# Moving the token blocks' reciprocals and products, and TensorE's transposes, to later units of an attention loop

## The chip, the cores and the metric

The kernel runs on one core of one Trainium2 chip. The metric is the device time of one execution in microseconds (us); lower is better. The core's engines work from instruction lists of their own and signal each other through semaphores: TensorE (PE in the profile; PEld are its weight loads), VectorE (DVE), ScalarE (ACT), GpSimd (POOL) and the transfer queue SyncE (SP).

## The reference, cut to what matters

```
x  : 8 x 512 tokens of 256 numbers;  xn = layernorm(x)
q, k, v = xn @ W_qkv.T                      16 heads of 16 numbers
qp, kp  = elu(q @ proj) + 1, elu(k @ proj) + 1     128 features a head
kv   = kp^T v  (per head, over the 512 tokens)     ksum = sum of kp
attn = (qp kv) / (qp ksum + 1e-8)
x + attn @ W_out.T + b_out + mixture of experts(xn)   8 experts, the best two of each token
```

The mixture of experts is the second half of the kernel and is not touched by the change.

## The kernel before, in words

The attention part goes through the 8 blocks of 512 tokens, one turn of a loop for each: block 0 is written out (`first=True`), blocks 1 to 6 are the turns of a loop, block 7 is `final_iteration`. Each engine has its own `iteration`, and a turn consists of 32 units, u = 0 to 31. Unit u makes one 128x512 piece of features: TensorE's `unit` multiplies it into PSUM bank F[u % 4] (L529 for the k features, u < 16, L535 for the q features), ScalarE's `exp` (L959) writes the exponential into the ring e_ring of four, and VectorE's `features` (L1355) combines both into kp or qp. TensorE's unit u waits until feature u-4 is done (semaphore `feat`), ScalarE's exp(u) also waits for feature u-4.

Everything else of the loop is hung between the units by hand, at an `if u == ...` of each engine. In turn b this is the state product of block b (`kv`, L547, 4 groups of 32 records, one for each 128 tokens), the projections of block b+1 (`qk_group` and `v_logits`, L473 to L475; `qk_rest`, L499, which subtracts the rounded part so that ScalarE's `qk_lo`, L938, can read what is left), and the end of block b-1: the attention result att_sb is transposed to tokens (`to_tokens`, L576, one for each of the four token blocks n = 0 to 3), VectorE takes the reciprocals of the denominators (`reciprocals`, L1361, 128x16) and multiplies (`products`, L1367, 128x256), and TensorE transposes back (`to_heads`, L583) and projects.

What ties these together are the PSUM banks that they share. `to_tokens(n)` writes the banks WK[1], DEN, WK[0], NUM for n = 0 to 3. `v_logits(b + 1, 0)` writes WK[1] and so waits for product 0 (`at_rdy` 4b-3), `kv(b, 0)` writes DEN and waits for product 1 (4b-2), `qk_group(b + 1, 1)` writes WK[0] and waits for product 2 (4b-1), `to_heads` needs all four products (4b). `to_tokens(b - 1, 3)` writes NUM and waits until `qk_lo(b + 1, 0)` has read it (`qkl_rdy` 4b+5). Feature 8 overwrites the kp half that `kv(b, 0)` reads, and waits for it (`kv_done`). On ScalarE, `qk_lo(b + 1, 0)` stands behind exp(11) and ahead of exp(12).

GpSimd sends the rows of block b to the experts' lists with eight indirect transfers (L1713) in each turn. They are paced by TensorE: transfer j waits until unit 2j is signalled (`f_full`, `TURN = 2`). SyncE loads x, xres and stores the result in the first third of a turn and rearranges kd and qd into Sk and Sq later.

Of the kernel before, what the change touches and what calls it, by code (L numbers as in the profile page):

```python
# [72 lines left out]
def build(nc, x, w_in, proj, w_out, b_out, experts, b1, b2, br, consts, out):  # L73
# [396 lines left out]
    def _(pe):  # L470
        def mm3(dst, wh_, wl_, mh_, ml_, first, last):

            nc.tensor.matmul(dst, wh_, mh_, start=first, stop=False)  # L473
            nc.tensor.matmul(dst, wh_, ml_, start=False, stop=False)  # L474
            return nc.tensor.matmul(dst, wl_, mh_, start=False, stop=last)  # L475
# [10 lines left out]
        def qk_group(b, i):  # L486

            pe.wait_ge(xtl_rdy, 2 * b + 2)
            col = (D, D + P, 0, P)[i]
            for k in range(KT):  # L490
                last = mm3(QK_BANK[i][:, :], WTh[:, k, col:col + P], WTl[:, k, col:col + P],
                           xTh[:, k, :], xTl[:, k, :], k == 0, k == KT - 1)
            last.then_inc(qk_full, 1)
# [8 lines left out]
        def v_logits(b, n):  # L502

            pe.wait_ge(xtl_rdy, 2 * b + 2)
            tok = slice(n * P, (n + 1) * P)
            for k in range(KT):
                last = mm3(V_BANK[n][:, 0:D + E], xTh[:, k, tok], xTl[:, k, tok],
                           WTh[:, k, 2 * D:QKVR], WTl[:, k, 2 * D:QKVR], k == 0, k == KT - 1)
            last.then_inc(v_full, 1)
# [29 lines left out]
        def kv(b, n):  # L539

            pe.wait_ge(feat, 32 * b + 4 * n + 4)
            if n == 0:
                pe.wait_ge(v_rdy, NT * b + NT)
            for c in range(4):
                for j in range(4):
                    h = 4 * c + j
                    last = nc.tensor.matmul(KV[32 * j:32 * j + 32, c * P:(c + 1) * P], vext[:, n, h, :],  # L547
                                            kp[:, n % 2, h * FEAT:(h + 1) * FEAT],
                                            start=n == 0 and c == 0, stop=n == NT - 1, skip_group_check=True)
            last.then_inc(kv_done, 1)  # L550
# [62 lines left out]
        def iteration(b, first=False):  # L613
# [4 lines left out]
            for u in range(32):  # L618
# [20 lines left out]
                    to_tokens(b - 1, 2)  # L639
                if u == 5:  # L640
                    qk_group(b + 1, 0)
                if u == 7:
                    if not first:
                        pe.wait_ge(at_rdy, 4 * b - 3)
                    v_logits(b + 1, 0)
                    if first:
                        pe.wait_ge(pos_read, 1)
                    else:
                        pe.wait_ge(at_rdy, 4 * b - 2)
                    kv(b, 0)  # L650
# [3 lines left out]
                if u == 13:  # L654
                    if not first:
                        pe.wait_ge(at_rdy, 4 * b - 1)
                    qk_group(b + 1, 1)
                    pe.wait_ge(qkl_rdy, 4 * b + 5)
                    if not first:
                        to_tokens(b - 1, 3)  # L660
# [534 lines left out]
    def _(dve):  # L1195
# [8 lines left out]
        def join():  # L1204
            dve.wait_ge(step, chain[0] + chain[1])
# [186 lines left out]
        def iteration(b, first=False, ahead=True):  # L1392
            for u in range(32):
                if u == 0:
                    norm_rows(b + 1, 0, 4)
                if u == 2:
                    tokens_lo(b + 1, 0)
                    tokens_lo(b + 1, 1)
                if ahead:
                    if u == 16:  # L1400
                        norm_stats(b + 2, 0, 2)
                    if u == 17:
                        norm_stats(b + 2, 2, 4)
                        join()
                    if u == 18:
                        norm_var(b + 2)
                    for i in STEPS_AT.get(u, ()):
                        norm_step(b + 2, i)
                if u == 27:
                    route_top(b + 1)  # L1410
                    route_mask(b + 1)
                    route_count(b + 1)
                if u == 28:
                    route_weights(b + 1)
                if u == 31:
                    numbers_of(b + 1)
                if not first:
                    if u == 3:
                        reciprocals(b - 1, 0)
                        reciprocals(b - 1, 1)  # L1420
                        products(b - 1, 0)
                    if u == 4:
                        products(b - 1, 1)
                    if u == 8:
                        reciprocals(b - 1, 2)
                    if u == 10:
                        products(b - 1, 2)
                    if u == 14:
                        reciprocals(b - 1, 3)
                        products(b - 1, 3)  # L1430
                    if u == 30:
                        residual(b - 1, 0)
                    if u == 31:
                        residual(b - 1, 1)
                if u == 31:
                    slots_of(b + 1)
                features(b, u)
# [383 lines left out]
```

## Time and profile before

| | us |
|---|---|
| median of 3 runs | 748.63 (747.15 to 756.17) |
| profiled execution | 756.15 |
| its span, first to last instruction | 754.0 |
| mean granted clock of TensorE | 0.986 |

| engine | busy us | share of the span |
|---|---|---|
| PE | 704.2 | 93% |
| PEld | 619.9 | 82% |
| DVE | 492.8 | 65% |
| ACT | 476.4 | 63% |
| POOL | 221.2 | 29% |

The page divides the span into 40 slices; the attention turns of the blocks 1 to 6 lie from about 66 to 287 us, and one turn takes 36.8 us. The views in order of time give the start of an instruction or of a merged group of equal ones, its length, engine, line, what it writes and reads, the count, and in brackets the idle time of the engine just before it with what ended that.

### The profile page before, as it was taken

What the parts mean: (1) busy time and instruction counts of PE and PEld (TensorE: products, weight loads), DVE (VectorE), ACT (ScalarE), POOL (GpSimd) and SP (SyncE); (2) the same over time, 40 slices, a digit from 0 to 9 for tenths busy, and PEclk for the clock granted to TensorE, in tenths of its full rate; (3) what the DMA queues carried; (4) which work ended last, traced back from release to release, by engine and by line L of the source; (5) the groups of instructions that cost most, each with busy time, mean ns of one, the idle gap of its engine ahead of it and who ended that gap; (6) DMA issues with size and microseconds to landing.
All of it is one profiled execution on the core that took longest, in us unless ns stands there. A gap on an engine that the chain in (4) does not pass through costs nothing.

```text
span 754.0 us, 17665 instructions
## 1 busy us (share of the span) xinstructions
PE 704.2 (93%) x5589; PEld 619.9 (82%) x5590; DVE 492.8 (65%) x1279; ACT 476.4 (63%) x879; POOL 221.2 (29%) x165
## 2 busy tenths in 40 slices
PE   3898999999999998799999999999999999999995
PEld 2675776767767675469999999999999999999995
DVE  7788888888889787936466464455656444456442
ACT  3587878686969696855556765546675444566551
POOL 0232323323232324522232422224222223322322
PEclk9899999999999999989999999999999999999998
DMA  7765464746473637643544642225445223443421
GB/s 232 183 185 143 116 197 113 204 106 205 104 211 98 183 98 214 219 156 89 139 88 87 155 150 50 43 44 101 150 76 154 43 52 69 82 112 86 59 43 22
DMA packets 50181, 91.64 MB, mean 122 GB/s; under 512 B 6897, under 2 KB 30193, under 8 KB 47873
## 3 DMA queue, kind: packets, MB, share of 16 engines
q1 hardware_dynamic: 34402, 59.36, 27.9%
q0 software_dynamic: 13872, 18.75, 14.3%
q10 hardware_dynamic: 1872, 13.11, 4.9%
q8 instruction: 17, 0.28, 0.2%
q14 instruction: 18, 0.15, 0.1%
HBM read 39.32 MB, written 26.67 MB: 88 GB/s over the span
## 4 chain that ended last, share of the span: by engine, by line
PE 64%; DVE 13%; issue 8%; ACT 8%; another core or an unknown queue 2%; DMA 1%; ACTq 1%; SPq 1%; DVEq 0%; POOLq 0%
PE F L473 9%; PE F L475 8%; PE F L474 8%; PE NUM L473 3%; PE F L529 3%; PE NUM L474 3%; PE NUM L475 3%; DVE qp L1355 3%; ACT h L1114 3%; ACT e_ring L959 3%; PE DEN L474 3%; PE DEN L473 3%; PE DEN L475 3%; PE F L535 2%; PE WK L567 2%
## 5 line engine op out<-in xcount | busy, mean ns | idle before, releaser
L1114 ACT ACTIVATE h<-F,b1c 128x384 f32<-128x384 f32 x200 | 110.8, 575 | 163.9 <-PE F L475 156.2
L1772 POOL DMA_INDIRECT out<-ysb,icur x75 | 120.0, 1599 | 303.7 <-DVE ysb L1616 288.9
L1593 DVE TENSOR_TENSOR hl<-h,hh 128x768 fp32r<-128x768 f32 x100 | 95.9, 959 | 156.7 <-ACT hh L1118 156.7
L959 ACT ACTIVATE e_ring<-F 128x512 f32<-128x512 f32 x256 | 145.3, 622 | 47.8 <-PE F L529 40.8
L473 PE MATMUL F<-gxh,wh 128*128 128x384 f32 (+1 forms) x400 | 129.8, 325 | 3.9 <-ACT h L1114 1.7
L475 PE MATMUL F<-gxh,wl 128*128 128x384 f32 (+1 forms) x400 | 128.4, 321 | 0.0
L474 PE MATMUL F<-gxl,wh 128*128 128x384 f32 (+1 forms) x400 | 128.4, 321 | 0.0
L1713 POOL DMA_INDIRECT xg<-rows,slots x64 | 63.2, 987 | 192.7 <-PE F L529 183.3
L1355 DVE SCALAR_TENSOR_TENSOR kp<-F,e_ring 128x512 f32<-128x512 f32 x128 | 82.5, 683 | 20.5 <-ACT e_ring L959 18.8
L1355 DVE SCALAR_TENSOR_TENSOR qp<-F,e_ring 128x512 f32<-128x512 f32 x128 | 85.3, 684 | 5.9 <-ACT e_ring L959 4.9
L1118 ACT ACTIVATE hh<-h 128x768 fp32r<-128x768 f32 x100 | 84.7, 847 | 3.3
L473 PEld LDWEIGHTS F<-gxh,wh 128*128 128x128 f32 x400 | 75.8, 190 | 9.1 <-issue 6.2
L474 PEld LDWEIGHTS F<-gxl,wh 128*128 128x128 f32 x400 | 75.9, 190 | 0.0
L475 PEld LDWEIGHTS F<-gxh,wl 128*128 128x128 f32 x400 | 75.8, 190 | 0.0
L529 PEld LDWEIGHTS F<-stacked_proj,Sk 97*128 97x128 f32 x256 | 37.3, 196 | 31.5 <-issue 15.2
L535 PE MATMUL F<-Sq,stacked_proj 97*128 97x512 f32 x128 | 54.0, 453 | 8.5 <-DVE qp L1355 5.6
L473 PE MATMUL NUM<-wh,hh 128*128 128x256 f32 x200 | 59.2, 296 | 1.8 <-DVE hl L1593 1.8
L529 PE MATMUL F<-stacked_proj,Sk 97*128 97x256 f32 x256 | 48.8, 310 | 8.7 <-DVE kp L1355 4.6
L473 PE MATMUL DEN<-wh,hh 128*128 128x256 f32 x200 | 56.6, 283 | 0.0
L474 PE MATMUL DEN<-wl,hh 128*128 128x256 f32 x200 | 56.6, 283 | 0.0
L475 PE MATMUL DEN<-wh,hl 128*128 128x256 f32 x200 | 56.6, 283 | 0.0
L475 PE MATMUL NUM<-wh,hl 128*128 128x256 f32 x200 | 56.4, 282 | 0.0
(220 smaller groups left out, 1572.6 us busy)
## 6 DMA issues: line engine op xcount, KB each, us to landing
wraw<-experts ACTq DMA_DIRECT2D x12, 1024.0 KB
grow<-xg SPq DMA_DIRECT2D x26, 408.0 KB
Sk<-kdh SPq DMA_DIRECT2D x64, 128.0 KB, 2.8
Sq<-qdh SPq DMA_DIRECT2D x64, 128.0 KB
xin<-x SPq DMA_DIRECT2D x8, 512.0 KB
Sk<-kdl SPq DMA_DIRECT2D x32, 128.0 KB, 2.5
Sq<-qdl SPq DMA_DIRECT2D x32, 128.0 KB
xres<-x SPq DMA_DIRECT2D x8, 512.0 KB
```

The source lines that it names most:

```text
L473: nc.tensor.matmul(dst, wh_, mh_, start=first, stop=False)
L474: nc.tensor.matmul(dst, wh_, ml_, start=False, stop=False)
L475: return nc.tensor.matmul(dst, wl_, mh_, start=False, stop=last)
L529: last = nc.tensor.matmul(F[c][:, s * D:(s + 1) * D], Sk[0:SROWS, pr, n * P:(n + 1) * P], stacked_proj[0:SROWS, 2 * pr:2 * pr + 2, :], sta ...
L535: last = nc.tensor.matmul(F[h % 4][:, :], stacked_proj[0:SROWS, h, :], Sq[0:SROWS, h // 2, :], start=True, stop=True)
L959: A(e_ring[:, u % 4, :], F[u % 4][:, :], ACT.Exp, bias=EXP_BIAS, scale=1.0 / DOWN).then_inc(exp_done, 1)
L1114: A(h32[:, m, :], F[m % 4][:, 0:T], ACT.Gelu, bias=b1c[:, w, m:m + 1]).then_inc(gelu, 1)
L1118: A(hh[:, 2 * q:2 * q + 2, :], h32[:, 2 * q:2 * q + 2, :], ACT.Copy).then_inc(hh_rdy, 1)
L1355: V.scalar_tensor_tensor(dst, F[u % 4][:, :], DOWN, e_ring[:, u % 4, :], ALU.max, ALU.min).then_inc(feat, 1)
L1593: V.tensor_tensor(hl[:, 2 * q:2 * q + 2, :], h32[:, 2 * q:2 * q + 2, :], f32(hh[:, 2 * q:2 * q + 2, :]), ALU.subtract).then_inc(hl_rdy, 1)
L1713: pool.indirect_dma_start(xg, bass.IndirectOffsetOnAxis(slots[:, k:k + 1], 0), rows[:, n, :], None, bounds_check=last_row, oob_is_err=Fals ...
L1772: pool.indirect_dma_start(out, bass.IndirectOffsetOnAxis(icur[:, s, :], 0), ysb[:, s, :], None, bounds_check=last_token, compute_op=ALU.ad ...
```

## The change

In VectorE's list of the blocks 1 to 6, the reciprocals of the token blocks 0 and 1 and product 0 move from ahead of feature 3 to ahead of feature 6, product 1 from 4 to 7, reciprocals 2 from 8 to 9, reciprocals 3 and product 3 from 14 to 17; product 2 stays at 10. In TensorE's list of the blocks 0 to 6, `v_logits(b + 1, 0)` moves from behind unit 7 to behind unit 8, `kv(b, 0)` from behind unit 7 to behind unit 9, and `to_tokens(b - 1, 3)` with its wait for `qk_lo` from behind unit 13 to behind unit 15. Nothing is added or removed, and block 7's turn stays.

```diff
--- before.py
+++ after.py
@@ -639,10 +639,11 @@
                     to_tokens(b - 1, 2)
                 if u == 5:
                     qk_group(b + 1, 0)
-                if u == 7:
+                if u == 8:
                     if not first:
                         pe.wait_ge(at_rdy, 4 * b - 3)
                     v_logits(b + 1, 0)
+                if u == 9:
                     if first:
                         pe.wait_ge(pos_read, 1)
                     else:
@@ -655,6 +656,7 @@
                     if not first:
                         pe.wait_ge(at_rdy, 4 * b - 1)
                     qk_group(b + 1, 1)
+                if u == 15:
                     pe.wait_ge(qkl_rdy, 4 * b + 5)
                     if not first:
                         to_tokens(b - 1, 3)
@@ -1415,17 +1417,17 @@
                 if u == 31:
                     numbers_of(b + 1)
                 if not first:
-                    if u == 3:
+                    if u == 6:
                         reciprocals(b - 1, 0)
                         reciprocals(b - 1, 1)
                         products(b - 1, 0)
-                    if u == 4:
+                    if u == 7:
                         products(b - 1, 1)
-                    if u == 8:
+                    if u == 9:
                         reciprocals(b - 1, 2)
                     if u == 10:
                         products(b - 1, 2)
-                    if u == 14:
+                    if u == 17:
                         reciprocals(b - 1, 3)
                         products(b - 1, 3)
                     if u == 30:
```

## Rows read from the trace of the kernel before

**Rows 1.** busy time by stretch, its columns and the stretch of blocks 1 to 6

```profile
core 0: us, PE busy (x) PEld busy (x) DVE busy (x) ACT busy (x) POOL busy (x), PEclk, DMA share, GB/s
...
66.00:287.00 221.00, 212.18 (x1947) 156.78 (x1945) 188.19 (x561) 171.52 (x366) 68.51 (x61) 1.00 0.55 152
```

**Rows 2.** TensorE in time, block 4's turn: start, length, line, operation, count, idle before

```profile
182.15 0.50 PE L529 MATMUL F<-stacked_proj,Sk 97*128 97x256 f32 x2 [0.58 <-DVE kp L1355]
...
183.31 1.08 PE L547 MATMUL DEN<-kp,vext 128*32 128x128 f32 x32
184.32 1.20 PE L529 MATMUL F<-stacked_proj,Sk 97*128 97x256 f32 x8
185.45 1.08 PE L547 MATMUL DEN<-kp,vext 128*32 128x128 f32 x32
186.46 0.50 PE L499 MATMUL NUM<-kdh,minus 128*128 128x512 f32 x1
...
189.24 0.65 PE L576 MATMUL NUM<-cst,att_sb 128*128 128x128 f32 x4 [0.32 <-ACT kdl L938]
...
190.54 1.10 PE L535 MATMUL F<-Sq,stacked_proj 97*128 97x512 f32 x2 [0.17 <-DVE kp L1355]
...
194.83 0.60 PE L583 MATMUL WK<-cst,at 128*128 128x128 f32 x4
```

**Rows 3.** VectorE in time, the same turn, same columns

```profile
180.97 0.26 DVE L1361 RECIPROCAL rec<-DEN 128x16 f32<-128x16 f32 x1 [0.77 <-PE WK L576]
181.14 0.36 DVE L1367 TENSOR_TENSOR at<-WK,rec 128x256 f32<-128x256 f32 x1
181.42 0.68 DVE L1355 SCALAR_TENSOR_TENSOR kp<-F,e_ring 128x512 f32<-128x512 f32 x1
...
182.34 2.48 DVE L1355 SCALAR_TENSOR_TENSOR kp<-F,e_ring 128x512 f32<-128x512 f32 x4
...
185.58 1.29 DVE L1355 SCALAR_TENSOR_TENSOR kp<-F,e_ring 128x512 f32<-128x512 f32 x2 [0.60 <-ACT e_ring L959]
...
189.80 1.29 DVE L1355 SCALAR_TENSOR_TENSOR kp<-F,e_ring 128x512 f32<-128x512 f32 x2 [1.40 <-ACT e_ring L959]
191.00 0.25 DVE L1361 RECIPROCAL rec<-NUM 128x16 f32<-128x16 f32 x1
...
194.07 0.74 DVE L1241 BATCH_NORM_STATS2 stats<-xin 128x6 f32<-128x256 f32 x2
```

**Rows 4.** ScalarE in time, the same turn, same columns

```profile
184.86 2.06 ACT L959 ACTIVATE e_ring<-F 128x512 f32<-128x512 f32 x4 [1.57 <-PE F L529]
188.59 0.60 ACT L938 ACTIVATE kdl<-NUM 128x512 fp32r<-128x512 f32 x1 [1.67 <-remote]
189.09 1.08 ACT L959 ACTIVATE e_ring<-F 128x512 f32<-128x512 f32 x2
```

**Rows 5.** GpSimd in time, the same turn, same columns

```profile
182.37 0.98 POOL L1713 DMA_INDIRECT xg<-rows,slots  x1 [2.19 <-PE F L529]
185.63 0.98 POOL L1713 DMA_INDIRECT xg<-rows,slots  x1 [2.27 <-PE F L529]
186.91 0.98 POOL L1713 DMA_INDIRECT xg<-rows,slots  x1 [0.30 <-issue]
```

**Rows 6.** waits over the whole run: waiter, releaser, us in total, times, longest

```profile
ACT kdl L938 <- remote: 9.9, 6, 1.7
...
DVE rec L1361 <- PE WK L576: 5.2, 6, 1.6
```

**Rows 7.** GpSimd in time, block 0's turn

```profile
41.57 0.99 POOL L1713 DMA_INDIRECT xg<-rows,slots  x1 [0.31 <-issue]
...
44.85 0.99 POOL L1713 DMA_INDIRECT xg<-rows,slots  x1 [0.30 <-PE F L529]
```

**Rows 8.** ScalarE in time, block 0's turn

```profile
43.28 0.60 ACT L938 ACTIVATE kdl<-NUM 128x512 fp32r<-128x512 f32 x1 [1.18 <-PE NUM L499]
...
45.21 2.10 ACT L959 ACTIVATE e_ring<-F 128x512 f32<-128x512 f32 x4
```

## The prediction

> **What bounds the kernel now.** Only the attention turns of the blocks 0 to 6 are edited, so I read, in this order: the busy time by stretch, to see which engine is full there; the timelines of TensorE, VectorE, ScalarE and GpSimd over one turn, to find TensorE's gaps and what ends each; the list of waits, to see that they come back in every turn. In the stretch of the blocks 1 to 6 TensorE is busy for 212.2 of 221.0 us and its clock is whole, 1.00 [rows 1]; VectorE has 188.2 and ScalarE 171.5. TensorE is the bound, and the change can only win what TensorE stands still, about 9 us in six turns, 1.5 a turn.
>
> In the turn of block 4 the stops are these. Unit 7 comes 0.58 late, for feature 3 [rows 2]. Feature 3 was late because VectorE stood for 0.77 ahead of reciprocal 1, for TensorE's `to_tokens` [rows 3]. Then `to_tokens(3)` comes 0.32 late, for ScalarE's kdl, and unit 16 0.17 late, for feature 12 [rows 2]. These two have one cause: ScalarE starts kdl at 188.59, after 1.67 of idleness [rows 4], though the matmul it waits for, `qk_rest`, ran from 186.46 to 186.96 by its record [rows 2]. The signal is 1.6 late. kdl stands ahead of exp(12) (189.09 [rows 4]), so feature 12 starts at 189.80 after 1.40 of idleness [rows 3], and unit 16 waits for it. The first wait is seen 6 times with 5.2 us in all, the second 6 times with 9.9 [rows 6]: once in each turn.
>
> What makes TensorE's signal late? The view names no source. GpSimd issues an indirect transfer in 0.98, and in this turn two of them stand back to back, 185.63 and 186.91, 0.30 apart [rows 5]; they are the transfers paced by unit 8 and unit 10, which TensorE makes in one stretch (184.32, 8 records [rows 2]). The second ends at 187.89, and the signal gets through at 188.59, 0.70 later. In block 0's turn a pair ends at 42.56 [rows 7] and kdl starts at 43.28, again after a long wait, 0.72 after that end [rows 8]. So the working reading is that a pair of issues back to back holds TensorE's signals back until some 0.7 after its end. Against it: the next pair of block 0 (the second from 44.85 to 45.84 [rows 7]) leaves the four exponentials from 45.21 on without a gap [rows 8]. The Trainium skill, Perfetto Trace Analysis, "Tensor Engine Instruction (MATMUL, LD_WEIGHTS)", says that the end of a matmul in a profile is computed and that the signal is pushed once PSUM has acknowledged the writes, outside of the record. By that alone the 1.6 would belong to the matmuls and would move with them; that is the second case below.
>
> **The change part by part.** The work is the same to the instruction, and no transfer of SP or POOL is moved in its list; only GpSimd's issues shift, since units pace them. All times are of block 4's turn.
>
> VectorE, features 3 to 7. The stop of 0.77 goes: reciprocal 1 now comes three features later, and its signal is there by 180.97. A feature takes 0.60 from start to start (0.62: 2.48 for four [rows 3]). Features 3 to 5 follow the second from 179.95 (180.97 less the stop and 0.25 for reciprocal 0) to 181.75. Then two reciprocals (0.17 to 0.26 apart) and product 0 (0.36, [rows 3]) end at 182.50, feature 6 starts at 182.45, product 1 ends at 183.45, feature 7 at 184.05.
>
> TensorE, units 7 to 9. Unit 7 starts at 181.57 (182.15 less 0.58), unit 8 at 181.85; a unit takes 0.28 (1.13 for four, 184.32 to 185.45 [rows 2]). `v_logits` then waits for product 0, until 182.55: a new wait of about 0.4, queued behind it unit 9 and `kv(0)`. Before it began at 182.49 (it takes 0.82 up to 183.31 [rows 2]). Unit 9 at 183.37, `kv(0)` at 183.65, which takes 1.01 (185.45 to 186.46), units 10 and 11, `kv(1)` at 185.22 instead of 185.45. Most of the 0.58 is paid back in the new wait: 0.23 is left.
>
> VectorE, features 8 to 12. Feature 8 waited for exp(8), which waited for unit 8 behind `kv(0)` (184.86, idle 1.57 [rows 4]), and began at 185.58 [rows 3]. Now unit 8 is early and feature 8 waits for `kv(0)` only: 184.8. Product 2 ends about 186.65, before `qk_group(1)` wants its bank at 187.0, so the moved reciprocal costs nothing there; feature 11 ends by 187.8, half a microsecond sooner.
>
> GpSimd. The transfer of unit 6 stays at 182.37 [rows 5]. Unit 8 is signalled at 182.1, so its transfer follows back to back, about 183.65 to 184.63. The one of unit 10 comes some 0.77 after its signal (as 184.86 to 185.63, [rows 4, 5]), at 185.75 or, if the new pair holds signals until 185.3, at 186.1; unit 12's at 187.7. The pair across `qk_rest` is gone. The new pair can hold the signal of `kv(0)`, to 185.3 instead of 184.8; that delays feature 8 by 0.5 and `qk_group(1)` by 0.1.
>
> The signal of `qk_rest` then comes at its record's end, 186.73: kdl from 186.75, exp(12) from 187.25, feature 12 from 187.9 to 188.6. TensorE is no longer stopped: `qk_group(1)` 187.05 to 188.55, units 14 and 15 (0.56), `to_tokens(3)` (0.43), unit 16 at 189.6 instead of 190.54. With these new waits about 0.9 is won a turn.
>
> Reciprocals and product 3. They stood between features 13 and 14 (191.00) and now follow the second pair of statistics (194.07, 0.74 long [rows 3]). Without them ahead that pair ends at 194.18, and product 3 at 194.9 (0.25 + 0.42), signalled at about 194.95; `to_heads` started at 194.83 [rows 2]. If feature 12 stays where it is, this costs 0.1 a turn; if feature 12 is 1.9 earlier, as above, product 3 is ready long before `to_heads` (now about 193.9), and the move costs nothing. Putting `to_tokens(3)` behind units 14 and 15 lets these cover its wait (0.32); where the wait is gone anyway, the move is worth nothing by itself.
>
> Block 0's turn has the same signal, kdl at 43.28, but no reciprocals; its part, below 0.5, I leave in the range. Blocks after 7 and the experts do not change.
>
> Sum: 6 turns x 0.9 = 5.4 us. Of the span of 754.0 that leaves 748.6, of the profiled 756.15 it leaves 750.8. That execution stood 7.5 above the median of the runs, 748.63; taken from the median the sum gives 743.2.
>
> **The rivals.**
>
> *The late signal stays late.* If it does not hang on the pair of issues, kdl moves only with `kv(1)`, by 0.23 at most, and feature 12 and unit 16 with it; product 3 takes back up to 0.1. For it: the pair of block 0 without effect [rows 7, 8], and the page's reading above. Against it: in both turns looked at the delay ends 0.70 to 0.72 after the end of an issue. Price: -0.23 to +0.1 a turn, 747.2 to 749.2; I take 748.5.
>
> *The signal comes later than now.* Place: kdl again. If the new pair (units 6 and 8) holds the signals of units 10 and 11 as well, the transfers of units 8, 10 and 12 can close up, and the last ends at 188.3, its hold at 189.0. kdl would come 0.45 later, unit 16 as much, and product 3 a further 0.1 behind `to_heads`: 0.55 x 6 = 3.3, 751.9. It decides from a kdl at about 188.5 on. For it: the three gaps in the new schedule are small, 0.3, 1.1 and 0.6 to 0.9. Against it: the lone issue of 182.37 to 183.35 [rows 5] goes by without harm to `kv(0)` at 183.31 and the unit behind it [rows 2].
>
> *All stops go.* TensorE then loses 0.23 as above and all of 0.32, 0.17 and the 0.16 or so which the bracketed gaps leave out, 1.1 to 1.3 a turn with 0.5 in block 0: up to 8 us, 740.6.
>
> **How the numbers follow.** The forecast, with kdl's signal in time, has 0.47; the late signal that stays 0.31; later than now 0.17; all stops gone 0.05. The time is 743.2. The likeliest case by itself runs from 741 to 746. The range reaches over the others: 740.5 below, and above 752, the price of the slower case, which leaves out its tail and runs like the one of 756.17. Two per cent (15 us) is about what a measurement of this kernel can tell from no change. No case reaches it: the whole of TensorE's idleness in the six turns is 9 us. Faster by over 2% has 0.02, slower 0.03, for a wait that I did not find; the rest, 0.95, is within.
>
> **What would show it right or wrong.** In the profile after: no idle time ahead of the second reciprocal; unit 7 at once behind unit 6; a wait of VectorE's product ahead of `v_logits`, 0.3 to 0.5; GpSimd's issues of units 6 and 8 back to back, those of units 8 and 10 apart; kdl with little idle time ahead of it and not named remote; feature 12 without its 1.40; unit 16 and `to_heads` without a wait. A turn should take 35.9 instead of 36.8. If the list of waits still has kdl with 1.6 six times, the reading of the signal was wrong; if `to_heads` waits for product 3, VectorE's last move was put too late.

## The result and the profile after

| | before | after |
|---|---|---|
| median of 20 runs each, us | 752.23 (747.15 to 756.46) | 748.99 (743.54 to 751.88) |
| profiled execution, us | 756.15 | 749.08 |
| its span, us | 754.0 | 747.0 |
| turns of the blocks 1 to 6, one by one, us | 38.38 36.80 36.83 36.79 36.81 36.71 | 37.43 36.39 36.45 36.40 36.32 35.55 |

The ratio is 0.9947, with an interval of 0.9927 to 0.9967: 0.5% faster, 3.2 us between the medians, where 5.4 were forecast and, from the median of three runs, 743.2 in all. The turns in the middle have become 0.40 us shorter, not 0.9; the first and the last of the six are 0.95 and 1.16 shorter, which makes 3.8 in all. (A turn is counted from one end-of-turn `attend` to the next. Outside of these six turns an execution also differs from the next: block 7 takes 38.5 to 43.9 us over the traces of this document, and 38.5 and 40.9 in two of one kernel, while all that follows the last `attend` takes 426.8 to 427.2 in every one. So the length of a turn is the sharper measure, and the runs below are read by it.)

Busy time by stretch, the blocks 1 to 6 of the kernel after, in the columns of [rows 1]:

```profile
core 0: us, PE busy (x) PEld busy (x) DVE busy (x) ACT busy (x) POOL busy (x), PEclk, DMA share, GB/s
62.50:282.00 219.50, 212.51 (x1967) 158.84 (x1960) 189.86 (x564) 173.28 (x368) 69.03 (x62) 1.00 0.56 155
```

TensorE still stands 7.0 us in them (219.50 less 212.51), where it stood 8.8 before. To see where, TensorE in time, block 4's turn; 3.97 is added to a start to compare it with [rows 2 to 5] (the code lines below TensorE's part have moved on by 2: features is L1357, the reciprocals L1363, the products L1369, exp L961, kdl L940, the transfers L1715):

```profile
177.23 0.85 PE L529 MATMUL F<-stacked_proj,Sk 97*128 97x256 f32 x6
178.75 0.40 PE L473 MATMUL WK<-WTh,xTh 128*128 128x264 f32 x1 [0.66 <-DVE at L1369]
...
179.92 1.08 PE L547 MATMUL DEN<-kp,vext 128*32 128x128 f32 x32
...
181.58 1.08 PE L547 MATMUL DEN<-kp,vext 128*32 128x128 f32 x32
182.59 0.50 PE L499 MATMUL NUM<-kdh,minus 128*128 128x512 f32 x1
...
184.79 0.63 PE L529 MATMUL F<-stacked_proj,Sk 97*128 97x256 f32 x4
185.26 0.60 PE L576 MATMUL NUM<-cst,att_sb 128*128 128x128 f32 x4
185.66 1.09 PE L535 MATMUL F<-Sq,stacked_proj 97*128 97x512 f32 x2
...
190.47 0.63 PE L583 MATMUL WK<-cst,at 128*128 128x128 f32 x4 [0.36 <-DVE at L1369]
```

The three stops of before [rows 2] are gone: units 6 to 8 run as one, `to_tokens(3)` and unit 16 follow without a wait. Unit 16 stands at 189.63 in the time of before, against 190.54. But there are two new stops, both for a product of VectorE: 0.66 ahead of `v_logits` (product 0) and 0.36 ahead of `to_heads` (product 3), which comes at 194.44 against 194.83. VectorE in time, the same turn:

```profile
177.99 0.25 DVE L1363 RECIPROCAL rec<-WK 128x16 f32<-128x16 f32 x1
178.15 0.19 DVE L1363 RECIPROCAL rec<-DEN 128x16 f32<-128x16 f32 x1
178.26 0.42 DVE L1369 TENSOR_TENSOR at<-WK,rec 128x256 f32<-128x256 f32 x1
...
181.44 0.69 DVE L1357 SCALAR_TENSOR_TENSOR kp<-F,e_ring 128x512 f32<-128x512 f32 x1 [1.22 <-PE DEN L547]
...
184.91 2.67 DVE L1357 SCALAR_TENSOR_TENSOR kp<-F,e_ring 128x512 f32<-128x512 f32 x4 [0.54 <-issue]
...
188.74 0.74 DVE L1243 BATCH_NORM_STATS2 stats<-xin 128x6 f32<-128x256 f32 x2
189.61 0.26 DVE L1363 RECIPROCAL rec<-NUM 128x16 f32<-128x16 f32 x1
189.90 0.42 DVE L1369 TENSOR_TENSOR at<-NUM,rec 128x256 f32<-128x256 f32 x1
```

Reciprocal 1 no longer waits. Feature 8 waits 1.22 for `kv(0)` (and no more for exp(8)), feature 12 0.54. ScalarE and GpSimd around the signal of `qk_rest`:

```profile
183.70 0.60 ACT L940 ACTIVATE kdl<-NUM 128x512 fp32r<-128x512 f32 x1 [1.13 <-PE NUM L499]
```

```profile
178.43 0.98 POOL L1715 DMA_INDIRECT xg<-rows,slots  x1 [1.39 <-PE F L529]
179.71 0.98 POOL L1715 DMA_INDIRECT xg<-rows,slots  x1 [0.30 <-issue]
182.25 0.98 POOL L1715 DMA_INDIRECT xg<-rows,slots  x1 [1.55 <-PE F L529]
```

The pair of transfers is now that of units 6 and 8, as forecast, and a lone transfer lies over `qk_rest`. kdl starts 1.11 after `qk_rest` (183.70 less 182.59); before it was 2.13 (188.59 less 186.46, [rows 4] and [rows 2]). The waits over the whole run show how often this comes back:

```profile
DVE kp L1357 <- PE DEN L547: 9.2, 7, 1.5
ACT kdl L940 <- PE NUM L499: 6.3, 6, 1.2
...
PEld WK L473 <- DVE at L1369: 4.9, 6, 0.9
...
PE WK L583 <- DVE at L1369: 2.5, 6, 0.6
```

kdl's six waits are those of block 0 and of the turns 2 to 6. Turn 1 has none, and is worth a look by itself. TensorE's `qk_rest` and `to_heads`, ScalarE's kdl and GpSimd's issues around `qk_rest`, turn 1 of the kernel after:

```profile
73.21 0.50 PE L499 MATMUL NUM<-kdh,minus 128*128 128x512 f32 x1
...
81.24 0.63 PE L583 MATMUL WK<-cst,at 128*128 128x128 f32 x4 [0.61 <-DVE at L1369]
```

```profile
73.75 0.60 ACT L940 ACTIVATE kdl<-NUM 128x512 fp32r<-128x512 f32 x1 [0.17 <-issue]
```

```profile
70.74 0.98 POOL L1715 DMA_INDIRECT xg<-rows,slots  x1 [0.31 <-issue]
73.26 0.98 POOL L1715 DMA_INDIRECT xg<-rows,slots  x1 [1.54 <-PE F L529]
```

Here no issue is under way when `qk_rest` starts (the last one ended at 71.72, the next begins 0.05 after), and kdl follows after 0.54. In the other turns a lone issue has begun 0.15 to 0.52 before `qk_rest`, and kdl follows 1.00 to 1.23 after it, 0.41 to 0.52 after the end of that issue. Even with kdl in time `to_heads` waits 0.61 for product 3 in turn 1.

### The profile page after: what moved, and what is told of

Read it like the earlier page. It is cut to its first block, busy times and chain, and to the rows that moved or that the text cites. A ratio compares the mean times of both kernels' runs of the same rounds, so it can differ in the third digit from the quotient of the medians.

```text
span 747.0 us, 17664 instructions
## 1 busy us (share of the span) xinstructions
PE 697.9 (93%) x5589; PEld 616.6 (83%) x5590; DVE 492.5 (66%) x1279; ACT 476.1 (64%) x879; POOL 220.9 (30%) x165
## 4 chain that ended last, share of the span: by engine, by line
PE 61%; DVE 17%; issue 11%; ACT 7%; DMA 1%; ACTq 1%; DVEq 1%; POOLq 0%; SPq 0%; another core or an unknown queue 0%
PE F L473 9%; PE F L475 9%; PE F L474 9%; PE NUM L473 3%; DVE qp L1357 3%; PE NUM L474 3%; PE NUM L475 3%; DVE kp L1357 3%; ACT h L1116 3%; PE DEN L473 3%; PE DEN L474 3%; PE DEN L475 3%; PE DEN L547 2%; PE F L535 2%; PE WK L473 2%
## 5 line engine op out<-in xcount | busy, mean ns | idle before, releaser
L961 ACT ACTIVATE e_ring<-F 128x512 f32<-128x512 f32 x256 | 146.0, 624 | 43.1 <-PE F L529 36.3
L1715 POOL DMA_INDIRECT xg<-rows,slots x64 | 63.1, 985 | 184.8 <-PE F L529 173.8
L1357 DVE SCALAR_TENSOR_TENSOR kp<-F,e_ring 128x512 f32<-128x512 f32 x128 | 82.7, 681 | 18.6 <-PE DEN L547 9.2
L1357 DVE SCALAR_TENSOR_TENSOR qp<-F,e_ring 128x512 f32<-128x512 f32 x128 | 85.3, 683 | 6.4 <-ACT e_ring L961 6.0
L474 PE MATMUL NUM<-wl,hh 128*128 128x256 f32 x200 | 56.4, 282 | 0.0
```

What stands on the lines that cost most here:

```text
L961: A(e_ring[:, u % 4, :], F[u % 4][:, :], ACT.Exp, bias=EXP_BIAS, scale=1.0 / DOWN).then_inc(exp_done, 1)
L1357: V.scalar_tensor_tensor(dst, F[u % 4][:, :], DOWN, e_ring[:, u % 4, :], ALU.max, ALU.min).then_inc(feat, 1)
L1715: pool.indirect_dma_start(xg, bass.IndirectOffsetOnAxis(slots[:, k:k + 1], 0), rows[:, n, :], None, bounds_check=last_row, oob_is_err=Fals ...
```

## The experiments

The theory after these traces: the first half of the change (TensorE's `v_logits` and `kv(0)`, VectorE's reciprocals and products 0 to 2) and the second (`to_tokens(3)`, product 3) each take a stop away and put a new one in, and what is gained hangs on how late TensorE's signals come. The rival: the transfers, which the change shifts, decide. A signal is called in time here when its reader starts 0.54 us after the start of the 128x512 matmul that it waits for, and late when it starts later. The runs were made on chips numbered 4, 2, 9 and 0, each beside the kernel before on the same chip. The chip of the two first traces has no number on record; it is called the first chip, since the kernel before takes some 16 us longer there than on any of these.

**e1 and f3: the first half alone** (chips 4 and 2). **e2 and f4: the second half alone.** e1 and f3 take from the diff everything but its second hunk and the move of reciprocals 3 and product 3; e2 and f4 take these two alone:

```diff
                     qk_group(b + 1, 1)
+                if u == 15:
                     pe.wait_ge(qkl_rdy, 4 * b + 5)
...
-                    if u == 14:
+                    if u == 17:
                         reciprocals(b - 1, 3)
                         products(b - 1, 3)
```

> Only the first half of the change: reciprocals 0 and 1, products 0 and 1, reciprocals 2 on VectorE, v_logits and the first state product on TensorE; to_tokens(3), reciprocals 3 and product 3 stay as before. Theory S (the gain is the signal of qk_rest, which comes early because unit 8 and with it GpSimd's transfer moved away from it): kdl's wait falls from 1.67 to 1.1 or less a turn, unit 16 comes 0.9 sooner, and to_heads has no wait for product 3, since that stands where it stood: -0.9 a turn of six, about 5.5 us, ratio 0.992 to 0.994, better than the whole change. Rival (both halves are needed, since to_tokens(3) behind unit 13 still stops for kdl): -0.4 a turn, ratio 0.996 to 0.998.

> Only the second half of the change: to_tokens(3) behind unit 15, reciprocals 3 and product 3 ahead of feature 17. Theory S: kdl keeps its late signal, 1.67 a turn, feature 12 stays where it is, and to_heads now waits 0.1 to 0.4 for product 3: no gain, ratio 1.000 to 1.003. Rival (covering to_tokens(3)'s wait is what counts): -0.3 a turn, ratio 0.997 to 0.998.

Measured on chip 4: the kernel before 736.42 (19 runs), e1 740.85, ratio 1.0055 (1.0032 to 1.0079); e2 740.90, 1.0055 (1.0027 to 1.0082). Each half alone makes the kernel slower; e1 was expected to gain 5.5. That could not be understood without the kernel before itself on such a chip, 16 us faster there than on the first one. So:

> The kernel before once more, for a trace on the same chip as the runs beside it: the runs of the four experiments so far had 736.4 for it instead of 752.2, and no late signals in any of their traces up to feature 12. Theory C (whether signals are late depends on the chip, and all of the gain came from them): if its median here is near 736, kdl starts within 0.1 of the end of qk_rest and a turn takes 34.7 to 35.0; if near 750, kdl is 1.6 late and a turn takes 36.8. Rival (the time between chips differs for another reason, in the experts' part): the turn is 36.8 in both.

> The changed kernel, on the same chip. Theory C: where the kernel before takes about 736, v_logits' new wait for product 0 and feature 8's new wait for the state product are all that is left of the change, with to_heads' wait for product 3, so it is slower, ratio 1.006 to 1.012, a turn 35.6 to 35.9; where the kernel before takes about 750, ratio 0.993 to 0.996 as measured. Rival (the change wins everywhere): ratio 0.993 to 0.996 in both.

> The first half of the change again. Theory C: where the kernel before takes about 736, 1.004 to 1.007 as measured; where it takes about 750, kdl's signal is 0.6 late instead of 1.6, to_heads doesn't wait for product 3, ratio 0.990 to 0.994. Rival (the first half loses on every chip, the gain being the second half's): 1.004 or more in both.

> The second half of the change again. Theory C: where the kernel before takes about 736, 1.004 to 1.008 as measured, all of it to_heads' wait for product 3; where it takes about 750, kdl stays 1.6 late, feature 12 stays, 1.000 to 1.003. Rival (the second half brings the gain there, by covering the wait of to_tokens(3)): 0.994 to 0.997 where the kernel before takes about 750.

Measured on chip 2: before 736.58 (23 runs); f2, the whole change, 745.12, 1.0108 (1.0078 to 1.0137); f3 741.38, 1.0051 (1.0028 to 1.0074); f4 739.12, 1.0031 (1.0008 to 1.0055). The turns: before 34.64, whole change 36.0, first half 35.3, second half 35.4. The stretch of the blocks 1 to 6 in the kernel before on this chip (f1):

```profile
60.20:268.40 208.20, 206.85 (x1954) 156.96 (x1958) 189.98 (x568) 174.32 (x369) 67.50 (x60) 1.00 0.58 161
```

TensorE stands 1.35 us in six turns, not 8.8: here there is next to nothing to win. Its ScalarE and its GpSimd at `qk_rest`, which starts at 177.70:

```profile
178.24 0.60 ACT L938 ACTIVATE kdl<-NUM 128x512 fp32r<-128x512 f32 x1
```

```profile
176.89 0.98 POOL L1713 DMA_INDIRECT xg<-rows,slots  x1 [1.44 <-PE F L529]
178.17 0.98 POOL L1713 DMA_INDIRECT xg<-rows,slots  x1 [0.30 <-issue]
179.46 0.98 POOL L1713 DMA_INDIRECT xg<-rows,slots  x1 [0.30 <-issue]
```

kdl starts 0.54 after `qk_rest`, with no idle time ahead of it, although three transfers stand back to back across it, 0.30 apart. So a pair of issues by itself does not hold a signal back: as a rule for every chip the working reading of the prediction is refuted. On the first chip its traces bear it out in a wider form, a lone issue being enough. The nearest comparison is one kernel in two traces: in f2's block 4 an issue begins 0.37 before `qk_rest` and kdl starts 0.54 after it; in the trace of after on the first chip the issue begins 0.34 before (182.25 and 182.59) and kdl starts 1.11 after. Now the whole change on chip 2 (f2), TensorE in time, its two stops:

```profile
177.68 0.39 PE L473 MATMUL WK<-WTh,xTh 128*128 128x264 f32 x1 [0.47 <-DVE at L1369]
...
189.24 0.63 PE L583 MATMUL WK<-cst,at 128*128 128x128 f32 x4 [0.61 <-DVE at L1369]
```

They stand at the same two places as in the trace of after on the first chip. The next table puts block 4's turn side by side, us from the turn's start:

| | before, first chip | after, first chip | before, chip 2 | after, chip 2 | first half | second half |
|---|---|---|---|---|---|---|
| reciprocal 1 | 8.28 | 9.43 | 7.43 | 9.22 | 9.22 | 7.43 |
| `v_logits(0)` | 9.80 | 10.02 | 8.96 | 9.81 | 9.81 | 8.96 |
| `kv(1)` | 12.76 | 12.86 | 11.91 | 12.65 | 12.65 | 11.91 |
| kdl | 15.90 | 14.98 | 13.46 | 14.20 | 14.20 | 13.46 |
| unit 16 | 17.86 | 16.93 | 16.14 | 16.70 | 16.79 | 16.05 |
| product 3 | 18.60 | 21.18 | 16.27 | 20.80 | 16.90 | 20.15 |
| `to_heads` | 22.14 | 21.75 | 19.95 | 21.38 | 20.59 | 20.72 |
| turn | 36.79 | 36.40 | 34.61 | 36.03 | 35.27 | 35.37 |

The first half costs 0.74 at `kv(1)` (the wait for product 0), the second 0.77 at `to_heads` (the wait for product 3), and the two add up. In the second half alone the wait is seen with its cause, TensorE and then VectorE:

```profile
187.73 0.63 PE L583 MATMUL WK<-cst,at 128*128 128x128 f32 x4 [0.61 <-DVE at L1368]
```

```profile
186.00 0.74 DVE L1242 BATCH_NORM_STATS2 stats<-xin 128x6 f32<-128x256 f32 x2
186.87 0.26 DVE L1362 RECIPROCAL rec<-NUM 128x16 f32<-128x16 f32 x1
187.16 0.42 DVE L1368 TENSOR_TENSOR at<-NUM,rec 128x256 f32<-128x256 f32 x1
```

Product 3 stands behind feature 16 and the second pair of statistics and ends at 187.58, 0.15 before `to_heads` can start.

**e3: the change with product 3 put at feature 15** (chip 4).

```diff
-                    if u == 17:
+                    if u == 15:
                         reciprocals(b - 1, 3)
                         products(b - 1, 3)
```

> The changed kernel with one edit: reciprocals 3 and product 3 ahead of feature 15 instead of 17. Theory S with the loss at to_heads: the wait of to_heads for product 3 (0.36 in block 4's turn) goes, the turn falls from 36.4 to about 36.05, 2.2 us in six turns below the changed kernel, ratio to before 0.991 to 0.992. Rival (to_heads' wait lies beside another that ends as late, the chain over ScalarE's qdh and exp(21)): no difference to the changed kernel, ratio 0.9945.

Measured: 742.86, ratio 1.0091 (1.0072 to 1.0110), turn 35.6; faster than before was expected. `to_heads` no longer waits, which wins 0.4 of the 0.75. The rest stays, because the reciprocal and product now stand ahead of feature 15, and unit 19 and what follows wait for that, 0.34 a turn: feature 16 starts at 19.67 of the turn, where it was at 19.25 in the first half alone and 19.06 in the whole change.

**g1: VectorE's moves of the first half without TensorE's. g2: TensorE's without VectorE's. g4: g2 with `to_tokens(3)` behind unit 15 and product 3 at feature 15** (chip 9, before 736.94 with 21 runs).

> Of the first half only VectorE's moves (reciprocals 0 and 1 and product 0 ahead of feature 6, product 1 ahead of 7, reciprocals 2 ahead of 9); v_logits and the state product stay behind unit 7. Theory W (what the first half costs where no signal is late is TensorE's wait for products 0 and 1): v_logits starts 9.8 after the turn's first attend, as in the changed kernel, instead of 8.96, the state product behind product 1 at about 11.0, and the units 8 to 11 follow it: second state product at 12.9 to 13.0 instead of 11.91, turn 35.6 to 35.8 where the kernel before has 34.6. Rival (feature 8's wait for the first state product is the cost, and comes from TensorE's move): turn 34.6 to 34.8.

> Of the first half only TensorE's moves (v_logits behind unit 8, the first state product behind unit 9), the products stay where they were. Theory W: products 0 and 1 are long done, TensorE doesn't wait, the second state product stays at 11.9, turn 34.6 where the kernel before has 34.6, ratio 0.999 to 1.001; on a chip with late signals unit 8's transfer leaves qk_rest, kdl comes 0.6 to 0.9 sooner, turn 35.7 to 36.0 instead of 36.8, ratio 0.993 to 0.995. Rival (the later state product holds feature 8): turn 0.2 or more longer than before without late signals.

> TensorE's moves of the whole change (v_logits 8, state product 9, to_tokens(3) behind unit 15), and of VectorE's only reciprocals 3 and product 3, one feature later than before (ahead of 15), since to_tokens(3) comes later. Theory W: without late signals 0.0 to 0.3 a turn longer than before (unit 16 waits for feature 12 in either order, to_heads has product 3 in time), ratio 1.000 to 1.003; with late signals -0.9 to -1.1 a turn, ratio 0.991 to 0.993. Rival (to_tokens(3) behind unit 15 costs by itself, through the wait of to_heads for qk_lo): 1.003 to 1.006 without late signals.

g1 took 739.89 (one run), turn 35.8; g2 738.97, ratio 1.0036 (1.0009 to 1.0064), turn 35.25; g4 742.16, 1.0080 (1.0054 to 1.0106), turn 35.6. The expectations of g2 (no wait) and g4 (at most 1.003) missed. In g1 `v_logits` waits 0.70 for product 0 and units 8 to 11 stay behind `kv(0)` besides, 1.1 a turn in all. In g2 the wait only changes its place, TensorE in time, block 4's turn:

```profile
173.20 0.50 PE L529 MATMUL F<-stacked_proj,Sk 97*128 97x256 f32 x2 [0.42 <-DVE kp L1356]
```

This is unit 8, made ahead of `v_logits`: it waits for feature 4, which stands behind the reciprocals and the products 0 and 1. Whichever engine gives way, units and products of this stretch do not both fit, and `kv(1)` is at 12.65 in g2 as in the whole change. In g4 `to_heads` is at 20.92, where e3 has 20.93: product 3 ahead of feature 15 costs the same 0.33 there. Only the order of before, `v_logits` and `kv(0)` ahead of unit 8, finds both ready.

**The transfers.** Four kernels move or lighten them with the order of before left alone. e4 sends all eight behind the units 16 to 23; h1 sends the last four behind units 16 to 22; h3 and i3 are one kernel twice, which sends the last four behind the units 12 to 15, so that none is issued between unit 7 and unit 12; h2 moves only one partition of 128 of x, xres and the result, and so leaves out most of the data.

```diff
# e4
-        pool.reg_mov(turn, 33)
+        pool.reg_mov(turn, 49)
...
-                        pool.wait_ge(f_full, 32 * b + 1 + TURN * (2 * n + r))
+                        pool.wait_ge(f_full, 32 * b + (1 + TURN * (2 * n + r) if b else 17 + 2 * n + r))
-            pool.reg_add(turn, turn, TURN if n + r < NT else 32 - TURN * (2 * NT - 1))
+            pool.reg_add(turn, turn, 1 if n + r < NT else 32 - (2 * NT - 1))
# h1, on that last line
+            pool.reg_add(turn, turn, 10 if r and n % 2 else TURN)
# h3 and i3, on that last line
+            pool.reg_add(turn, turn, (2, 2, 2, 6, 1, 1, 1, 17)[2 * n + r])
# h2, the same for xres and for the stored rows
+            rows_ = slice(0, P if isinstance(b, int) else 1)
-            sp.dma_start(xin[:, :, :], x_rows[b]).then_inc(x_ld, 16)
+            sp.dma_start(xin[rows_, :, :], x_rows[b][rows_]).then_inc(x_ld, 16)
```

> The kernel before, with GpSimd's eight indirect transfers of a block paced by the units 16 to 23 instead of 0, 2, .. 14 (blocks 0 to 6; block 7 as before), the rest untouched. Theory P (GpSimd's issues hold TensorE's signals): kdl starts within 0.3 of the end of qk_rest instead of 1.6, VectorE's wait for to_tokens is gone, a turn takes 35.6 to 36.0 instead of 36.8, ratio 0.991 to 0.994, unless signals are now held in the second half. Rival M (the matmuls themselves end later than their records say): kdl still starts 1.6 after the record of qk_rest, with the transfers elsewhere; ratio 0.999 to 1.003. Rival L (the loads of x and xres in flight hold them, the transfers don't): the same as M for kdl.

> The kernel before; of GpSimd's eight transfers of a block the first four stay with the units 0 to 6, the last four go to the units 16 to 22 instead of 8 to 14 (blocks 1 to 6). The loads of x and xres are in flight as before. Theory P (issues of GpSimd hold TensorE's signals where the chip does this at all): on a chip with late signals kdl starts within 0.3 of the end of qk_rest instead of 1.6 and the turn takes 35.6 to 35.9 instead of 36.8, and a late signal shows between units 16 and 22 instead. Rival L (the loads hold them): kdl stays 1.6 late. On a chip without late signals the turn stays at 34.6 to 34.9 and this says nothing of P.

> The kernel before, but of x, xres and the result only one partition of 128 is moved in the turns of the blocks 1 to 6, so the output is wrong and the experts get other rows; GpSimd's transfers untouched. Only the attention turns are read. Rival L: on a chip with late signals kdl and reciprocal 1 are on time, turn 34.6 to 35. Theory P: both stay late, 36.8. On a chip without late signals 34.6 in either case, and later than that would show a cost of the transfers' traffic itself.

> The kernel before with GpSimd's last four transfers of a block paced by the units 12, 13, 14, 15 instead of 8, 10, 12, 14, so that none is issued between unit 7 and unit 12, where qk_rest signals; loads untouched. Theory P: on a chip with late signals kdl starts within 0.3 of the end of qk_rest, turn 36.0 or less instead of 36.8. Rival L (the loads in flight): 1.6 late, 36.8. On a chip without late signals 34.6 to 34.9.

> The kernel before, with the transfer of unit 8 sent two units later and the last three transfers one unit apart, so that a lone transfer no longer precedes qk_rest back to back. Nothing is left out. On a chip where the kernel before takes about 752 us: if the pair of transfers makes the signal late, kdl has no late signal and the turn is 35.2 to 35.6; if it does not, the turn stays at 36.8. On a chip where the kernel before takes about 736 us it tells nothing new: 34.64 a turn either way.

e4 (chip 4) took 752.52, ratio 1.0214 (1.0181 to 1.0246), turn 37.0 to 37.9; h1 (chip 9) 768.59, one run, turn 41.0. Both expectations missed. h2 (chip 2) 738.62, h3 (chip 2) 732.78 and i3 (chip 0) 736.69, each one run, with 735.97 and 733.14 for the kernel before beside them: all three have turns of 34.6, like before. Those chips signal in time, so these three say nothing on what makes the signals late on the first one; they do say that neither the weight of the loads nor the place of those four transfers has a price of its own. h3 and i3, the same kernel, differ by 3.9 us, none of it in the turns of the blocks 1 to 6: i3 has 1.4 more ahead of them and 2.4 more in block 7 (40.9 and 38.5 us from its start to its last `attend`).

h1 lost 6.4 a turn. Where 3.7 of them went is seen on VectorE and on GpSimd:

```profile
206.28 3.83 DVE L1262 SCALAR_TENSOR_TENSOR rtmp<-rtmp,var 128x4 f32<-128x4 f32 x1
```

```profile
206.75 2.36 POOL L1700 TENSOR_TENSOR xres<-xres,bo_bc 128x1024 f32<-128x1024 f32 x1
209.04 1.05 POOL L1707 COPY rows<-xn 128x1024 f32<-128x1024 f32 x1
```

A four-column instruction of VectorE that takes 0.15 elsewhere in this trace lasts 3.83 and ends at 210.11, with the second of GpSimd's two instructions (210.09). The late transfers push these two, which follow them on GpSimd, from the stretch in which VectorE makes features and statistics into that of the small Newton steps, whose operands all lie in SBUF. e4 has the same, 3.44 for such a step in place of 0.15. The other 2.7 of h1's turn come later in it and were not followed to a cause. The Trainium skill, SBUF — State Buffer, "Terms", says that VectorE and GpSimd share one pair of SBUF ports, lock-allocated and held for the full instruction, so that the loser blocks; the trace agrees, with 3.83 against 0.15, and shows the loser as a long instruction, begun by its record 0.47 ahead of GpSimd's add, and not as a wait. In f1 the same add of GpSimd (2.40 from 182.72) lies over statistics of 0.74 and features of 0.67 to 0.69, their usual lengths.

**d2: the change on a chip that signals in time, with late signals put in by hand** (chip 2), and **i1: the same for the kernel before** (chip 0). d2 has work of about 0.4 on VectorE ahead of feature 8 and 0.6 on ScalarE ahead of kdl; i1:

```diff
             act.wait_ge(qkr_full, 4 * b + i + 1)
+            if i == 0 and not isinstance(b, int):
+                act.wait_ge(b2_ld, 16)
+                A(b2bc[:, 0:1024], b2bc[:, 0:1024], ACT.Copy)
+                A(b2bc[:, 1024:1682], b2bc[:, 1024:1682], ACT.Copy)
...
             dve.wait_ge(tok_full, NT * b + n + 1)
+            if n == 1 and not isinstance(b, int):
+                dve.wait_ge(b2_ld, 16)
+                V.tensor_tensor(b2bc[:, 1682:2048], b2bc[:, 1682:2048], b2bc[:, 1682:2048], ALU.max)
+                V.tensor_tensor(zrows[:, :], zrows[:, :], zrows[:, :], ALU.max)
```

> The changed kernel with the two stops of its own first trace added by hand in the loop's turns: about 0.41 on VectorE ahead of feature 8, once the state product's signal is there, and 0.57 on ScalarE ahead of kdl. Theory C: the turn takes 36.3 to 36.5 where the changed kernel alone has 36.0, as in its first trace; 36.0 plus almost nothing would mean that the changed order has slack there and its first trace was slow elsewhere.

> The kernel before, with work of its own put where the first profile showed a signal of TensorE late: in the blocks 1 to 6 VectorE runs two idle operations (about 0.45 and 0.35 us) ahead of reciprocal 1, and ScalarE two copies of 1024 and 658 columns (about 1.6 us together) ahead of kdl. Nothing is left out. Theory (the 36.8 us turn of the first profile is the 34.64 us turn plus those two late signals, each of which is passed on to TensorE): a turn of 36.6 to 36.9 us, with unit 7 and unit 16 behind their features. Rival (the slow turn of the first profile came from elsewhere, and the late signals were a by-product): 34.7 to 35.6, since TensorE has 0.8 and 1.3 us of other work ahead of what waits. On a chip whose TensorE signals late as well, add 0.3 to 1.0.

i1 took 748.67 beside 733.14 for the kernel before. Its turn is 36.70 us, where the kernel before has 34.64 on such chips and 36.80 on the first one. Its ScalarE and its TensorE, block 4's turn:

```profile
183.18 1.06 ACT L940 ACTIVATE b2bc<-b2bc 128x1024 f32<-128x1024 f32 x1
184.15 0.74 ACT L941 ACTIVATE b2bc<-b2bc 128x658 f32<-128x658 f32 x1
184.79 0.58 ACT L942 ACTIVATE kdl<-NUM 128x512 fp32r<-128x512 f32 x1
```

```profile
178.33 0.50 PE L529 MATMUL F<-stacked_proj,Sk 97*128 97x256 f32 x2 [0.46 <-DVE kp L1359]
...
185.42 0.66 PE L576 MATMUL NUM<-cst,att_sb 128*128 128x128 f32 x4 [0.31 <-ACT kdl L942]
...
186.72 0.50 PE L535 MATMUL F<-Sq,stacked_proj 97*128 97x512 f32 x1 [0.17 <-DVE kp L1359]
```

These are the three stops of [rows 2], 0.58, 0.32 and 0.17, to 0.12 us, made by two delays of known length. Each event of the table above lies 0.10 to 0.14 before that of the first trace (kdl 15.80 and 15.90, unit 16 17.73 and 17.86, turn 36.68 and 36.79). So the two late signals are the whole of what the first chip loses in each of the turns 2 to 5. The outer turns differ: in turn 1 the first chip's stop at unit 7 is 1.51 and i1's 0.47 (turns of 38.38 and 37.35), and in turn 6 i1 has ScalarE's delay alone (35.65, against 36.71 on the first chip and 34.31 without delays). d2 took 744.7, turn 36.21, where f2 had 36.01 and the first chip 36.40: 0.2 of the 0.4 between them are those two signals, 0.2 is missing, about as much as a third late signal of that trace, which d2 left out: ScalarE waits 0.35 for the token transposes of x, where f2 has 0.15, and feature 2 comes at 6.87 of the turn, where d2 and f2 have 6.67.

## Why the prediction was right or wrong

**What bounds the kernel: right for the first chip, and no more than that.** TensorE's stops of 1.5 a turn, and the three places with their two causes, were read rightly, and i1 made them out of two delays. That the stops would be there on any chip was taken for granted. On chips that signal in time they are 1.35 us in all six turns.

**The stop at unit 7 and the new wait for product 0: mechanism right, the size missed.** Forecast 0.4 and `kv(1)` 0.23 earlier; measured 0.66, and `kv(1)` at 185.55 in the time of before, 0.10 later. Of this difference of 0.33, `v_logits` itself came 0.17 late (182.72 against 182.55), behind a token transpose of x whose signal came 0.2 later in this trace. The terms of this sum were each near the truth; the result was a small difference of two of them.

**Feature 8: right.** It waits for `kv(0)` and not for exp(8). It came at 185.41 in the time of before, where 184.8 or, if signals are held, 185.3 was written. The held case is the one that came: it starts 0.75 after the end of the second issue of the new pair (180.69), and 1.52 after `kv(0)`'s start, where f2 has 1.15.

**The signal of `qk_rest`: the step failed by 0.6.** The forecast had kdl at 186.75. It came at 187.67, and of this 0.92 a part of 0.35 is that `qk_rest` itself ran at 186.56 and not at 186.2. The rest is the signal: 1.11 from start to start, where chip 2 has 0.54. The term put at nothing was a lone issue. The pair was gone, but unit 10's transfer, forecast from 185.75 or 186.1, was issued from 186.22 to 187.20 in the time of before, over `qk_rest`, and kdl came 0.47 after its end. That a lone issue does no harm had been read from `kv(0)` behind the one of 182.37; turn 1, where no issue was under way when `qk_rest` started, has kdl in time. The case "the late signal stays late" was half right as well: it fell from 1.6 to 0.6.

**Unit 16: right, with nothing to spare.** Forecast 189.6, measured 189.63. kdl came 0.9 late and still in time: it ends at 184.30, 0.5 before TensorE is through with `qk_group(1)` and begins unit 14 (184.79), so `to_tokens(3)` would not have waited in its old place either. Feature 12, forecast 1.9 earlier, came 0.93 earlier and ended 0.05 ahead of unit 16. That the move of `to_tokens(3)` is "worth nothing by itself" agrees with chip 2, where it brings unit 16 from 16.14 to 16.05; with a kdl as late as before it was not tried.

**"The move of product 3 costs nothing": this step failed, and it decides the size.** Forecast was a product 3 at 193.0 (194.9 less 1.9) and a `to_heads` at 193.9, so 0.9 of slack. In f2, with kdl in time, there is none: product 3 ends 5.81 after feature 12 begins (183.28 to 189.09), where 5.1 was reckoned, and TensorE would have been at `to_heads` after 5.35 (189.24 less the wait of 0.61), where 6.0 was. Two errors of 0.7, one on either side, and 0.15 from the product's end to the start of `to_heads` turned 0.9 of slack into 0.6 of wait. The first: taking reciprocal and product out from between features 13 and 14 was to bring all behind them forward by 0.67, but feature 14 then stood 0.49 for its exponential, and reciprocals 3 another 0.12. The second: in f2 unit 16 comes 1.29 after feature 12, where 1.7 was reckoned, and TensorE would have reached `to_heads` 4.07 after unit 16, where the 4.3 of before, with unit 17 waiting for feature 13, had been carried over. On the first chip the way there was another: TensorE was at `to_heads` at 194.08 in the time of before, close to the 193.9 written, and product 3 ended at 194.29 instead of 193.0, 0.97 of it from the late kdl and 0.3 from what lies behind feature 12. But turn 1 of that trace, with kdl in time, waits 0.61 as f2 does: kdl's signal alone would not have saved the step. The prediction's last sentence named this wait as the sign of a last move put too late, and that is what e3, f4 and the table show.

**The sum.** Four of the six turns gave 0.4 each, not 0.9: 0.5 went at `to_heads` (0.93 won at unit 16, 0.39 left behind it). With the outer two it is 3.8 us, where 5.4 was written. And 743.2 started from 748.63, the median of three runs; with 20 runs the kernel before is at 752.23. Of the 5.8 us by which 748.99 lies above the forecast, 3.6 are this base and 2.2 the smaller gain (3.2 and not 5.4 between the medians). The two traces differ by 7.0, more than the medians, since the profiled execution of before was among its slowest: 2.2 lie ahead of block 1, 3.8 in the six turns, 0.9 in block 7.

**The rivals.** No transfer held kdl's signal longer than before. The case in which all stops go has a wrong sum: its parts make 0.88 a turn, and not 1.1 to 1.3. The rival on the slower side happened on the other chips, by another mechanism than the one written down: not kdl, but the two products of VectorE. What was not considered is that the order of before might already fit a chip on which the signals come in time; there it leaves 1.35 us of stops, and every one of the seven reorderings tried costs 0.6 to 1.4 a turn.

**What stays open** is why GpSimd's issues go with late signals on the first chip and not on the others. In its two traces the link is close. Of 14 starts of kdl (block 0 and six turns, twice), 13 have an issue under way when `qk_rest` starts, and are late: 0.67 to 0.72 after the end of the second issue of a pair (before), 0.41 to 0.52 after that of a lone one (after). The one without is in time. On the chips 2, 4, 9 and 0 kdl starts 0.53 or 0.54 after `qk_rest` with issues at the same place, wherever no delay was put in. But this is read from two traces and was not tested by an edit on the first chip, since the later runs fell on others. That it is the chip, and not the hour or some other condition of those runs, is not shown either.

## What to carry to other kernels

An idle time whose waiter starts well after the releaser's record has ended may belong to the chip and not to the order of the kernel; find it again on a second chip before reordering a kernel for it. Where one engine is 99% busy in a stretch, each step that it waits for must be checked with its own slack, and a change that frees this engine from one producer shortens the slack of all later ones: here more than half of what had been won at unit 16 (0.54 of 0.93) was lost again at `to_heads`. And moving a long GpSimd instruction is a change to VectorE's list too.

## What the runs showed of the hardware

- ScalarE's reader of one 128x512 matmul started 0.54 us after the matmul's start on chip 2 (f2), and 2.13 (before) and 1.11 (after) on the first chip; the same kernel took 752.23 on the first chip and 736.4 to 736.9 (medians of 19 to 23 runs) on three others, at the same granted clock of 1.00 in the stretch (f1, e1, g2). The Trainium skill, Perfetto Trace Analysis, "Tensor Engine Instruction (MATMUL, LD_WEIGHTS)", has the signal pushed once PSUM acknowledges the writes. The 0.6 to 1.6 us more on the first chip are shown by its two traces alone.
- In these two traces such a signal is late where an indirect issue of GpSimd (0.98 us) is under way at the matmul's start, and in time (0.54) in the one turn where none is; on the four other chips it is in time beside such issues too.
- Two delays of 0.74 and 1.61 us in the lists of VectorE and ScalarE, neither of them the bound, cost 2.06 a turn together (i1), nearly their sum of 2.35; ScalarE's alone cost 1.34 (turn 6 of i1, 35.65 against 34.31).
- A VectorE instruction of four columns lasted 3.83 us beside GpSimd's add and copy, instead of 0.15 (h1).
